# Entries of the second and the third expert layer, by blocks inside the attentions in front of them, with the third's shared second product in fp32

## The reference

```python
x = x + tanh(g_xattn[i]) * attention_i(layernorm(x), ctx_2048, ...)
x = x + tanh(g_ffn[i])   * ffn_i(layernorm(x), ...)
# L1 attention: linear, 16 heads, elu-like feature map, sigmoid gate
# L1 ffn: 8 experts (inner 512), top 2, ternary weights, activations rounded to 8 bits (step = max|x| / 127)
# L2 attention: softmax, 32 query heads on 8 groups
# L2 ffn: shared expert  silu(x @ Ws1) * (x @ Wsg) @ Ws2   (inner 256)
#         + 7 routed experts of the same form, top 3 by softmax(x @ gate_w + gate_b) + biases
```

## Time and profile before

| | us |
|---|---|
| median of 3 runs | 1164.59 (1162.75 to 1167.77) |
| the profiled execution | 1170.64 |
| its span, first to last instruction | 1168.8 |
| TensorE busy | 908.0 (78%) |
| VectorE busy | 792.0 (68%) |
| ScalarE busy | 611.9 (52%) |
| GpSimd busy | 447.9 (38%) |

### The profile page before, as it was taken

One profiled execution on the slowest core, in us unless ns is written; L12 is line 12 of the kernel. 1 busy time (PEld: TensorE's weight loads), 2 busy tenths in 40 slices (PEclk: granted clock), 3 DMA queues, 4 the chain that ended last, 5 costly groups with the idle time before them and its releaser, 6 DMA issues.

```text
span 1168.8 us, 20420 instructions
## 1 busy us (share of the span) xinstructions
PE 908.0 (78%) x5870; PEld 682.0 (58%) x5885; DVE 792.0 (68%) x2045; ACT 611.9 (52%) x1393; POOL 447.9 (38%) x520
## 2 busy tenths in 40 slices
PE   5778789969999657778688989868797888925386
PEld 3557689957777343444455655547586777613254
DVE  6745648858886776778588877646654353289885
ACT  3654357745443485778556556554245343304564
POOL 3167624430000115665454544530256576505200
PEclk9988989979999897999899999989899999955599
DMA  9854457763200021222540020020152522350001
GB/s 285 140 164 146 145 176 220 233 223 113 73 15 1 28 64 48 58 62 56 179 154 20 10 64 1 1 92 8 28 170 83 159 78 86 104 176 1 1 19 55
DMA packets 95971, 109.19 MB, mean 93 GB/s; under 512 B 14269, under 2 KB 85842, under 8 KB 95874
## 3 DMA queue, kind: packets, MB, share of 16 engines
q1 hardware_dynamic: 84162, 76.76, 22.4%
q0 software_dynamic: 11712, 31.20, 8.4%
HBM read 73.89 MB, written 34.03 MB: 92 GB/s over the span
## 4 chain that ended last, share of the span: by engine, by line
PE 49%; DVE 13%; issue 11%; ACT 9%; POOL 4%; another core or an unknown queue 2%; DMA 2%; ACTq 0%; DVEq 0%; SPq 0%; POOLq 0%
PE bank L3272 5%; PE bank L1582 3%; PE bank L2731 3%; PE bank L3296 2%; PE bank L2772 2%; POOL f_sorted L1275 2%; PE bank L2326 2%; PE bank L1608 2%; PE bank L2765 2%; PE bank L1901 2%; PE bank L1926 1%; PE bank L3632 1%; PE bank L2706 1%; PE bank L2334 1%
## 5 line engine op out<-in xcount | busy, mean ns | idle before, releaser
L3017 POOL DMA_INDIRECT f_got<-f_tokens,f_places x54 | 55.7, 1032 | 71.3 <-DVE f_places L946 55.1
L3178 DVE TENSOR_TENSOR f_act<-f_silu,bank 128x256 f32<-128x256 f32 x54 | 22.7, 421 | 81.9 <-ACT f_silu L3079 51.2
L3023 POOL DMA_INDIRECT f_outputs<-f_y,f_places x54 | 55.2, 1021 | 50.5 <-ACT f_y L3093 40.0
L1282 POOL DMA_INDIRECT f_outputs<-f_y,f_places x39 | 41.3, 1058 | 57.9 <-ACT f_y L1332 35.9
L2515 POOL TENSOR_TENSOR work<-work 128x512 f32<-128x512 f32 x32 | 33.0, 1063 | 76.1 <-ACT work L2563 76.1
L2085 POOL DMA_INDIRECT f_got<-f_tokens,f_places x39 | 40.8, 1046 | 55.1 <-DVE f_places L946 37.8
L2635 DVE TENSOR_REDUCE work<-bank 128x8 f32<-128x512 f32 x64 | 43.5, 680 | 16.3 <-PE bank L2731 16.0
L2093 POOL DMA_INDIRECT f_outputs<-f_y,f_places x39 | 38.9, 998 | 39.8 <-ACT f_y L2148 30.9
L2639 DVE TENSOR_TENSOR work<-bank,work 128x512 f32<-128x512 f32 x64 | 44.3, 692 | 3.6 <-ACT work L2601 1.4
L3079 ACT ACTIVATE f_silu<-bank 128x256 f32<-128x256 f32 x54 | 20.9, 388 | 48.4 <-PE bank L3272 40.1
L2326 PE MATMUL bank<-tern,f_xq 128*128 x146 | 44.7, 433 | 1.9 <-issue 1.8
(11 more groups left out here) (552 smaller groups left out, 3220.3 us busy)
## 6 DMA issues: line engine op xcount, KB each, us to landing
f_back<-f_outputs SPq DMA_DIRECT2D x21, 256.0 KB, 4.8
f_back<-f_outputs SPq DMA_DIRECT2D x10, 512.0 KB, 6.3
f_got<-f_sorted SPq DMA_DIRECT2D x39, 129.0 KB
f_sorted<-clear_row SPq DMA_DIRECT2D x1, 4992.0 KB, 27.3
raw<-in_L_ffn_w SPq DMA_DIRECT2D x24, 176.0 KB
tern_raw<-in_L_ffn_gate_w SPq DMA_DIRECT2D x8, 512.0 KB
tern_raw<-in_L_ffn_up_w SPq DMA_DIRECT2D x8, 512.0 KB
tern_raw<-in_L_ffn_down_w SPq DMA_DIRECT2D x8, 512.0 KB
```

The lines of the kernel that those rows point to most:

```text
L1282: pool.indirect_dma_start(g.outputs, bass.IndirectOffsetOnAxis(ap=dest[:, j:j + 1], axis=0), y_out[:, j % OUT_RING, :], None).then_inc(gon ...
L3017: pool.indirect_dma_start(got[:, j % GATHERS, :], None, tokens, bass.IndirectOffsetOnAxis(ap=sorter.token[:, j:j + 1], axis=0)).then_inc(s ...
L3023: pool.indirect_dma_start(outputs, bass.IndirectOffsetOnAxis(ap=sorter.dest[:, j:j + 1], axis=0), y_out[:, j % OUT_RING, :], None).then_in ...
```

## The change

Expert layer 2: blocks 0, 1 and 2 are aggregated, normalized, rounded and (0 and 1) cast within steps 11 to 16 of attention 2, in four buffers instead of two. The cast of the rows moves from VectorE to ScalarE. Behind the attention remain block 3's norm and rounding, the cast of blocks 2 and 3, all transposes and logits. Expert layer 3: blocks 0 to 2 are normalized, and blocks 0 and 1 turned and split, within steps 48 to 69 of attention 3; the shared weights, the tokens' stores and the routing weights go there too. In the shared expert the second product takes the hidden product and the loaded weights as they are, in fp32: no split of either. The sorting chain's order beside it is written anew, with TensorE's ranks in front of unit 2 and its three inverse products in front of units 5 to 7.

```diff
@@ layer1_attention
+            ENTRY_MEANS, ENTRY_SHIFTS = {11: 0, 13: 1}, {12: 0, 14: 1}
+            ENTRY_NORMS, ENTRY_ROUNDS, ENTRY_ROWS = {13: 0, 14: 1, 15: 2}, {14: 0, 15: 1, 16: 2}, {15: 0, 16: 1}
...
@@ gpsimd, behind the last pair of deviations
+                for g in range(2):
+                    layer1_entry.deviations(pool, g)
@@ scalar, end of step t
+                    if t in ENTRY_NORMS:
+                        layer1_entry.norm(act, ENTRY_NORMS[t])
+                    if t in ENTRY_ROWS:
+                        layer1_entry.rows(act, ENTRY_ROWS[t])
@@ vector, end of step t
+                    if t in ENTRY_ROUNDS:
+                        layer1_entry.round(dve, ENTRY_ROUNDS[t])
+                    if t in ENTRY_MEANS:
+                        layer1_entry.means(dve, ENTRY_MEANS[t])
+                    if t in ENTRY_SHIFTS:
+                        layer1_entry.shift(dve, ENTRY_SHIFTS[t])
@@ layer1_experts
-            through = (xn, ctx_sb)
+            through = (ctx_sb, middle[0], middle[1], xn)
+            GROUPS = (slice(0, 2 * BT), slice(2 * BT, 3 * BT), slice(3 * BT, TILES))
...
+            def entry_norm(act, i):
+                g = max(0, i - 1)
+                act.wait_ge(norm.rstd, norm.all_there - TILES + GROUPS[g].stop)
+                act.wait_ge(p.shift, g + 1)
                 for k in range(BT):
                     t = i * BT + k
-                    act.activation(through[i % 2][:, k, :], X[:, t, :], ACT.Identity, scale=ln_rstd[:, t:t + 1],
+                    act.activation(through[i][:, k, :], X[:, t, :], ACT.Identity, scale=ln_rstd[:, t:t + 1],
...
+            def entry_round(dve, i):
...
+                if i >= 2:
+                    dve.wait_ge(p.kept[i % 2], 16)
+                    dve.wait_ge(p.rowed, i - 1)
...
+            def entry_rows(act, i):
+                act.wait_ge(p.entry, i * 5 + 5)
+                act.wait_ge(p.rounded, (i + 1) * BT)
...
+                act.activation(row_out[:, i % 2, :, 0:D // 2].bitcast(BF16), rounded[:, i % 2, :, :], ACT.Copy, bias=-MAGIC).then_inc(p.rowed, 1)
@@ scalar of layer1_experts
+                entry_rows(act, 2)
+                for i in range(2):
+                    scalar_turned(act, i)
+                router.scalar_logits(act, 0)
+                entry_norm(act, 3)
+                router.scalar_keep(act, 0)
+                for i in range(2, BLOCKS):
+                    scalar_turned(act, i)
+                    router.scalar_logits(act, i - 1)
+                    router.scalar_keep(act, i - 1)
+                router.scalar_logits(act, BLOCKS - 1)
                 router.scalar_keep(act, BLOCKS - 1)
+                entry_rows(act, 3)
@@ layer2_attention
-            WEIGHTS_AT = {1: (0,), 2: (1,), 3: (2,), 5: (3,), 6: (4,), 7: (5, 6)}
+            WEIGHTS_AT = {1: (0,), 2: (1,), 3: (2,), 5: (3, 4), 6: (5,), 7: (6,)}
...
+                for x in range(2):
+                    layer2_entry.tokens(sp, x)
+                sp.wait_ge(s.score, UNITS // PAIRS)
+                layer2_entry.sync(sp)
+                layer2_entry.tokens(sp, 2)
...
+            ENTRY_MEANS, ENTRY_SHIFTS = {48: 0, 56: 1}, {56: 0, 62: 1}
+            ENTRY_NORMS = {57: (0, 2), 58: (2, 4), 59: (4, 6), 60: (6, 8), 65: (8, 12)}
+            ENTRY_TURNS = {59: (0, 0), 62: (0, 1), 64: (1, 0), 65: (1, 1)}
+            ENTRY_HIGHS = {60: ((0, 0),), 63: ((0, 1),), 66: ((1, 0), (1, 1))}
+            ENTRY_LOWS = {61: ((0, 0),), 65: ((0, 1),), 69: ((1, 0), (1, 1))}
+            ROUTE_AT = 65
@@ layer2_experts
+            RANKS_AT = 2
...
+            def entry_shared_high(act):
+                act.wait_ge(p.shared, LOADS)
+                act.activation(shi[:, :], raw_s[:, 0:DOWN_AT], ACT.Copy).then_inc(p.hi0, 1)
...
@@ scalar of layer2_experts
+                for c in range(DC):
+                    entry_high(act, AHEAD - 1, c)
+                entry_shared_high(act)
+                router.scalar_logits(act, 0)
+                router.scalar_keep(act, 0)
+                for t in range(AHEAD * BT, TILES):
+                    entry_norm(act, t)
+                router.scalar_logits(act, 1)
...
-                    act.wait_ge(p.hid, u + 1)
-                    if u >= 2:
-                        act.wait_ge(p.down, u - 1)
-                    act.activation(whole_hi[:, u % 2, :], act_s[:, u % 2, :], ACT.Copy).then_inc(p.ahi, 1)
@@ vector of layer2_experts
-            def vector_whole_low(dve, u):
...
                 def between(x):
-                    if x < 3:
-                        vector_hidden(dve, x)
-                    else:
-                        vector_whole_low(dve, x - 3)
+                    if x in (1, 2):
+                        vector_hidden(dve, x - 1)
                 sorter.vector_choose(dve, between)
...
@@ tensor of layer2_experts
-                    for a, w in ((whole_hi, shi), (whole_hi, slo), (whole_lo, shi)):
...
+                    mm = pe.matmul(bank[4 + k // 2][:, k % 2 * D:k % 2 * D + D], act_s[:, u % 2, k * P:(k + 1) * P], down_w(raw_s, q),
+                                   start=q == 0 and k % 2 == 0, stop=q == IC - 1, skip_group_check=True)
...
                 for u in range(UNITS + 1):
+                    if u == RANKS_AT:
+                        sorter.tensor_ranks(pe)
+                    if UNITS - K <= u < UNITS:
+                        sorter.tensor_inverse(pe, u - (UNITS - K))
                     if u < UNITS:
                         tensor_up(pe, u)
-                    if u == 3:
-                        sorter.tensor_ranks(pe)
-                    if u == UNITS:
-                        sorter.tensor_inverse(pe, K - 1)
                     if u:
                         tensor_down(pe, u - 1)
...
-                hold(pe, p.hid, UNITS)
-                hold(pe, p.copied, 2 * BLOCKS)
...
+                        if i < 2:
+                            hold(pe, p.copied, 2 * BLOCKS - 1 + i)
```

More of the change, by code:

```diff
@@ L2096, in gpsimd, with entry_means @@
                         gather(j + LEAD)
[L2098 to L2102 removed]
+            def entry_means(dve, g):
+                tiles = GROUPS[g]
+                dve.wait_ge(norm.stat, STATS + SEEN[g])
+                for t in range(tiles.start, tiles.stop):
+                    dve.bn_aggr(ln_mv[:, t, :], ln_stat[:, t, :]).then_inc(norm.stat, 1)
@@ L2985, in tensor_summary @@
                 pe.wait_ge(m.kept, 4)
-            def sync(sp):
-                router.sync(sp)
-                sp.wait_ge(*before)
-                load(sp, [io[name] for name in ("L2_ffn_Ws1", "L2_ffn_Wsg", "L2_ffn_Ws2")], raw_s[:, :], p.shared)
-                for i in range(BLOCKS):
-                    sp.wait_ge(norm.xn, (norm.first + i) * BT + BT)
-                    sp.dma_start(tokens.rearrange("(i k p) d -> i p k d", k=BT, p=P)[i], through[i % 2][:, :, :]).then_inc(p.kept[i % 2], 16)
+            AHEAD = BLOCKS - 1
@@ L2994, in sync @@
+            layer2_entry.sync, layer2_entry.norm, layer2_entry.tensor = entry_sync, entry_norm, entry_tensor
+            layer2_entry.high, layer2_entry.low = entry_high, entry_low
+            layer2_entry.means, layer2_entry.deviations, layer2_entry.shift, layer2_entry.tokens = entry_means, entry_deviations, entry_shift, sync_tokens
+            layer2_entry.weights = router.vector_weights
+            def sync(sp):
+                sync_tokens(sp, AHEAD)
                 sp.wait_ge(s.up, 2)
```

291 lines of the change are left out of this document (166 added, 125 removed).

## The result

| | before | changed |
|---|---|---|
| median of 14 runs each, us | 1168.28 | 1157.90 |
| profiled execution | 1170.64 | 1160.70 |
| its span | 1168.8 | 1158.9 |

The ratio is 0.991, 95% interval 0.9889 to 0.9931: faster by 0.9%, some 10 us. The forecast was 1147 us against the first three runs of before (1164.59), a ratio of 0.985. So the sign was right and the size was not: the sum of -17.55 us stands against -9.9 us between the two profiled executions. 1157.9 lies 0.9 us above the stated range. Part of that is where the forecast stood: the median of all 14 runs of before is 3.7 us above that of its first three, and 0.991 of 1164.59 would be 1154.1.

The account below looks back on a forecast made before the run. No engine is full, so each stage has its own bound, VectorE's chain in the shared expert. Terms -0.25 (expert layer 2 in all), +3.0, -11.3 and -9.0 sum to -17.55 us: 1153.1 profiled, forecast 1147 us, range 1139 to 1157.

Parts of the forecast that it names:

- Attention 2, +6.3: Attention 2's end: three TensorE waits of 1.5, 1.5 and 2.65 us plus 0.6 for the third rounding, +6.3 us.
- rival (d): Both attentions' ends: ScalarE's new work stalls TensorE so its clock halves; 28 us more, 1175 us in all; chance 0.06.
- Entry of expert layer 2, -6.9: Last addition of attention 2 to the choice of experts: 17.5 us against 24.4, -6.9 us (-5.4 to -8.4).
- +0.35 for the row cast: Expert layer 2: block 3's row cast on ScalarE ahead of 24 copies of turned weights costs +0.35 us.
- Attention 3, +3.0: Attention 3: moved normalizations and transposes lengthen steps 58 to 60 by 1.0, 0.5 and 1.5; +3.0 us (+1.0 to +5.0).
- Entry of expert layer 3, -11.3: Last addition of attention 3 to the choice of experts: 12.15 us against 23.45, -11.3 us (-9 to -12.5).
- Shared expert, -9.0: Expert layer 3, choice to first routed product: near 41.4 us instead of 50.4, -9.0 us (-5 to -10.5).
- four take 0.86 us, 0.215 each: Price of 256-column f32 matmuls, read in attention 2: a shared-expert unit takes 0.86 us instead of 1.44, TensorE 4.6 shorter.
- rival (c): Shared expert: four passes per f32 matmul, routed stage starts near 45 us instead of 41.4; 1151 us; chance 0.05.
- (a): Attention 2 takes the new work better: only its chain pays, 2.6 us instead of 6.3; 1143 us; chance 0.13.
- (b): Shared expert: 2.7 us of new TensorE idle time ahead of the ranks drops the clock, +4; 1151 us; chance 0.15.
- (e): Some early entry piece waits for a late one and holds an in-order queue; half the gain gone, 1157 us; chance 0.09.

Follow-up runs that it names:

- low_parts_later: The changed kernel, but POOL starts the shared weights' low parts only after VectorE's block 3 shifts; ratio to the kernel before 0.9899.
- Experiment 8: Also old_entry_2: the changed kernel with attention 2 and expert layer 2 as in the kernel before; ratio to the kernel before 0.9904.
- experiment 1: Same run as low_parts_later: the changed kernel, with POOL's low parts of the shared weights waiting for block 3's shifts; ratio to the kernel before 0.9899.
- Experiment 3: Also half_down: the changed kernel, but the shared expert's fp32 second product makes only 128 of its 256 columns; ratio to the kernel before 0.9895.
- norms_behind_copy: The changed kernel, but in attention 2 ScalarE's normalizations and row casts stand behind the attended tile's copy; ratio to the kernel before 0.9863.
- rounding_later: As norms_behind_copy, with VectorE's rounding of block 1 a step later and of block 2 behind the last addition; ratio to the kernel before 0.9843.
- old_shared: The changed kernel with expert layer 3's shared expert as before (split second product, old order); ratio to the kernel before 0.9937.
- ranks_behind_unit_2: As low_parts_later, with TensorE's 17 rank matmuls moved behind the up products of unit 2; ratio to the kernel before 0.9862.
- split_new_order: As low_parts_later, keeping the new order, but the shared second product in three split passes with low parts on VectorE; ratio to the kernel before 0.9961.
- low_parts_on_pool: As low_parts_later, but the shared second product in three split passes with hidden values' low parts on POOL; ratio to the kernel before 0.9963.
- experiment 4: Same run as old_shared: the changed kernel with expert layer 3's shared expert as in the kernel before; ratio to the kernel before 0.9937.
- experiment 7: Same run as low_parts_on_pool: low_parts_later with a split shared second product, its hidden low parts on POOL; ratio to the kernel before 0.9963.

## Why the prediction was right in sign and wrong in size

**Attention 2, +6.3.** The mechanism and all three waits were right; the stretch grew by 8.0. By steps, between additions, it grew by 2.5, 2.1, 3.4 and 0.1 us for 1.5, 1.5, 2.65 and 0.6. Where the clock kept up to the third wait (low_parts_later) it was 1.5, 1.5, 3.4 and 0.1, so the fall behind the first wait is worth 1.5. Two other terms were off and offset each other in part, which is luck: the third wait's by 0.8, as the clock fell behind that wait in every kernel with it, and the rounding's 0.6, of which 0.1 came. I had priced the clock only as rival (d), all or nothing, at 28 us. The term should have been a wait and, with some chance, the half clock behind it.

**Entry of expert layer 2, -6.9.** Measured 24.42 to 17.55 us, -6.9. The +0.35 for the row cast did not come either: from the choice to the first turned token pass 23.86 us (435.17) for 23.79. Experiment 8 agrees that attention 2 and this entry together are worth nothing that its interval shows.

**Attention 3, +3.0.** Measured +3.2.

**Entry of expert layer 3, -11.3.** Measured -6.0. This is the largest miss. The step that failed is "POOL's deviations are early or beside it; POOL's low part ... ends before the shared products start": I asked whether POOL would be in time, not whom it holds up. It held the shift, 1.7 us, which lies on the chain (experiment 1). The other 3.6 us are the clock at half from 781 on, which I had not put into any case for this stretch; three of the four kernels with the same entry did not have it, so that part is this execution's. (In the prediction's own sums, 386.45 + 0.48 is 386.93 and the four terms of this entry make 12.2; neither moves the forecast.)

**Shared expert, -9.0.** Measured -6.1. The step that failed is "four take 0.86 us, 0.215 each". The row counts four instructions, but the code at its line issues two matmuls: TensorE carries one fp32 matmul out as two rows. Each of the 32 costs 0.43 us, a unit 1.72, and TensorE gets 2.3 us longer instead of 4.6 shorter. This is rival (c), to which I gave 0.05: it put the routed stage "near 45" us behind the choice, and it came at 44.3. Experiment 3, with the 0.86 for a unit that I had assumed, brings back 41.0. The Trainium skill (FP8 and Floating Point Precision, TensorE Precision Notes) counts four passes for true FP32. The trace agrees after all, roughly: 0.43 us is 3.6 times the 0.12 of a split pass. I had used a wrong count of rows to overrule it.

**The rivals.** (a) did not come in any run. (b) did not come in the changed kernel, where TensorE waited only 1.28 us ahead of the ranks (801.75). Elsewhere it is real, but a matter of the execution: with waits of 2.06 to 2.08 us there the clock fell in low_parts_later and old_entry_2 and did not in norms_behind_copy and rounding_later; a fall costs 1.5 us (45.2 against 43.7, two kernels each). (c) came. (d) came in small: 364 to 384 shows 0.91 of the clock, above its sign of 0.8. (e) left no trace: attention 3 grew as forecast. Of the signs, the choice of expert layer 2 came at 411.31 and the attentions grew by 11.2 us, under 12; but the clock was at its lower level for the first 3 us of the shared stage (791.5 to 794.4), which I had named as a sign of being wrong.

Put together in profiled executions: -17.55, with +1.7 in attention 2, +5.3 in the entry of expert layer 3, +2.9 in the shared expert and +0.2 in attention 3, is -7.5. Against -9.9, 2.4 us are left: 1.2 that the changed execution was ahead at 357, and the rest in small differences between 411 and 735 and behind the first routed product, whose causes stay open. The 1.2 is within what executions differ by there: in kernels whose code is the same up to that addition it stands between 354.5 and 358.2.

Open is what decides whether the clock falls behind a wait. In attention 2, kernels with the same steps and the same waits of 1.48 us fell in step 14 (the changed kernel), in step 15 (half_down, old_shared, ranks_behind_unit_2, split_new_order) or in neither (low_parts_later, low_parts_on_pool). And in the entry of expert layer 3 the changed kernel and rounding_later fell behind waits of at most 1.01 us, with which half_down, norms_behind_copy and old_entry_2 kept the clock.

## What to carry to other kernels

Count the matmuls in the code at a row's line before dividing the row's time by its count. When work is moved onto an idle engine, ask what it locks for others, and put filler work of an in-order engine behind the instruction that somebody waits for, not ahead of it: that placing alone took attention 2's stretch from 36.3 to 31.0 us, 1.5 of it the clock. After a move, look for the engine that is next: in the shared expert it was TensorE after VectorE, and the stage took 44.3 us where VectorE's chain alone was forecast at 41.4.

## What the runs showed of the hardware

A short VectorE instruction can be held for the whole length of a GpSimd one: 0.16 us became 2.33 when it began 0.07 us behind a GpSimd subtraction, and stayed 0.16 when it began 0.03 us ahead (experiment 4). It works both ways (GpSimd's 1.26 us became 2.58, experiment 7). The Trainium skill (SBUF — State Buffer, Who interferes with whom) says the same, that the two share a pair of ports under an exclusive lock and that the one that starts first keeps it for its whole instruction; the trace agrees, with the held instruction ending within 0.03 us of the other (778.87 and 778.84).

TensorE's clock fell behind waits of 1.5 to 3.5 us, not each time, and in the entry of expert layer 3 also behind waits of 0.8 and 1.0 us, in two kernels of the five that have them. In the changed kernel it stayed there at 1.2 GHz from 781 to 794.5, until the shared expert's run without waits had begun.
